# Query tiles with two blocks ahead, even slots of maxima, and a first phase loaded from the stage ahead

## The reference

```python
h = tok(x, ...)                       # attention in shifted 4x4 windows, 8 heads, with a relative table
h = h + attn(layernorm(h), ...)       # full attention over all 3136 tokens of an image, 8 heads of 32:
    q, k, v = split(x @ qkv_w + qkv_b)
    attn = softmax(einsum('bnhd,bmhd->bhnm', q * scale, k) + bias[rel_idx])
    out = einsum('bhnm,bmhd->bnhd', attn, v) @ proj_w + proj_b
h = h + ffn(layernorm(h), ...)        # gelu feed-forward for the half of the tokens with the top gate values
```

## Time and profile before

| | |
|---|---|
| median of 3 runs | 6077.67 us (6074.65 to 6080.56) |
| profiled execution | 6058.31 us, its span 6056.4 us |
| TensorE busy in the span | 5790.5 us (96%) |
| VectorE busy | 4380.1 us (72%) |
| GpSimd busy | 4386.0 us (72%) |
| ScalarE busy | 3273.6 us (54%) |
| mean granted clock of TensorE | 0.979 of 2.4 GHz |
| products for scores (line 1141) | 5600 |
| products for maxima (line 1205) | 5600 |

### The profile page before, as it was taken

How to read it: one execution, slowest core, us unless ns; L and a number is a source line. 1 busy time by engine, 2 the same in 40 slices (tenths; PEclk the granted TensorE clock), 3 DMA queues, 4 the chain that set the end, 5 groups by cost and what they waited for, 6 DMA issues and landing times. The chain is left out here.

```text
span 6056.4 us, 121185 instructions
## 1 busy us (share of the span) xinstructions
PE 5790.5 (96%) x37698; PEld 3429.1 (57%) x37698; DVE 4380.1 (72%) x8484; ACT 3273.6 (54%) x6740; POOL 4386.0 (72%) x1475
## 2 busy tenths in 40 slices
PE   5999998999999999999999999999999999984899
PEld 4777776555555555555555555555555555533566
DVE  4777776777877777777777777777777777736540
ACT  3555454266666666666666666666666666652222
POOL 2444444588888888888888888888888888875453
PEclk9999999799999999999999999999999999997899
DMA  2323223211011111101101110111111000015442
GB/s 73 100 93 105 95 98 112 62 35 37 16 37 33 28 25 37 36 17 37 33 27 25 37 36 17 37 33 27 25 37 36 16 17 17 15 31 160 119 98 44
DMA packets 197572, 297.79 MB, mean 49 GB/s; under 512 B 38038, under 2 KB 162334, under 8 KB 193998
## 3 DMA queue, kind: packets, MB, share of 16 engines
q1 hardware_dynamic: 181958, 269.42, 15.8%
q0 software_dynamic: 12432, 19.38, 1.6%
q10 hardware_dynamic: 2680, 2.63, 0.1%
HBM read 167.63 MB, written 124.50 MB: 48 GB/s over the span
## 5 line engine op out<-in xcount | busy, mean ns | idle before, releaser
L1302 DVE TENSOR_REDUCE tops<-ps_m 128x1 f32<-128x448 f32 (+1 forms) x5600 | 3116.7, 616 | 899.3 <-PE ps_m L1205 863.5
L1278 ACT ACTIVATE prob<-ps_s 128x448 f32<-128x448 f32 (+1 forms) x5600 | 2613.1, 548 | 1739.3 <-PE ps_s L1141 1696.8
L1111 POOL TENSOR_TENSOR tile_sum<-prob 128x1792 f32<-128x1792 f32 x448 | 1803.2, 4025 | 647.2 <-ACT prob L1278 646.8
L1141 PE MATMUL ps_s<-queries,keys 97*128 97x448 f32 (+1 forms) x5600 | 2197.3, 397 | 12.5 <-ACT prob L1278 7.6
L1205 PE MATMUL ps_m<-keys,queries 96*128 96x448 f32 (+1 forms) x5600 | 2090.1, 380 | 28.1 <-DMA keys<-k_parts 25.6
L1111 POOL TENSOR_TENSOR tile_sum<-tile_sum,prob 128x1792 f32<-128x1792 f32 x448 | 1808.0, 4036 | 31.8
L1141 PEld LDWEIGHTS ps_s<-queries,keys 97*128 97x128 f32 (+1 forms) x5600 | 1041.4, 187 | 1152.9 <-ACT prob L1278 661.4
L1157 PE MATMUL ps_o<-prob,values 128*32 128x448 f32 x11200 | 1341.8, 551 | 3.0 <-ACT prob L1278 1.2
L1205 PEld LDWEIGHTS ps_m<-keys,queries 96*128 96x128 f32 (+1 forms) x5600 | 1061.2, 190 | 234.1 <-DVE tops L1302 89.5
L1157 PEld LDWEIGHTS ps_o<-prob,values 128*32 128x32 f32 x11200 | 226.5, 108 | 379.4 <-issue 245.0
L1169 PE MATMUL ps_d<-tile_sum,ones 128*32 128x448 f32 x3584 | 420.9, 541 | 3.3 <-POOL tile_sum L1111 3.3
(11 more groups left out here) (181 smaller groups left out, 4096.3 us busy)
## 6 DMA issues: line engine op xcount, KB each, us to landing
queries<-q_parts SPq DMA_DIRECT2D x288, 160.0 KB, 3.3
keys<-k_parts SPq DMA_DIRECT2D x96, 392.0 KB, 7.1
xT<-in_x SPq DMA_DIRECT2D x56, 224.0 KB, 2.6
hidden_and_bias<-base SPq DMA_DIRECT2D x28, 448.0 KB, 3.1
q_parts<-hi SPq DMA_DIRECT2D x56, 224.0 KB, 1.9
q_parts<-lo SPq DMA_DIRECT2D x56, 224.0 KB, 1.9
k_parts<-hi SPq DMA_DIRECT2D x56, 224.0 KB, 1.9
k_parts<-lo SPq DMA_DIRECT2D x56, 224.0 KB, 1.9
```

The lines of the kernel that those rows point to most:

```text
L1111: nc.gpsimd.tensor_tensor(tile_sum[k % 2][:, :, :], left, prob[:, t % SLOTS, :, :], ALU.add).then_inc(summed, 1)
L1141: mm = nc.tensor.matmul(o[:, 0:CH], keys[x.u][:, j, at:at + k], queries[x.v][:, j, own:own + CH], start=True, stop=not last, skip_group_ch ...
L1278: nc.scalar.activation(prob[0:k, t % SLOTS, j, :], ps_s[0:k, score_bank(x.hm, i), 0:CH], ACT.Exp).then_inc(exp_done, 1)
L1302: nc.vector.tensor_reduce(tops[0:rows, j, r - blocks[0], c:c + 1], ps_m[0:rows, e % MB, 0:CH], AX.X, ALU.max).then_inc(m_used, 1)
```

## The change

It has two parts.

1. The tile of queries is 6 blocks wide, four of its own and `MORE` = 2 ahead; the first two blocks of a group are done for all four heads from the tile ahead, the others pair by pair. The spills are 8, 24, 12, 28, 16, 32 and 20, which gives 100 maxima to every slot (80 to the last of the last phase). The opening fill has 120 maxima instead of 122.
2. Keys, queries and corner of the first phase are allocated outside the two stages (`FirstPhase`), and SP loads them in the windowed stage: in round 27 the queries behind job 0, the corner behind job 1, and the keys of heads 0 and 1 behind jobs 2 and 3; in round 28 the keys of heads 2 and 3 behind jobs 0 and 1. The attention stage loads only the values itself. To make room, `ident` is gone; the first 128 columns of `out[0]` serve to make `ident_r`, and the turns' transposes read `ident_r`.

The diff, cut to its core:

```diff
+BLK = 128
+OWN, MORE = 4, 2
+AHEAD = (OWN + MORE) * BLK
...
+            def first_queries(pair):
+                rows = slice(2 * pair * DH, 2 * (pair + 1) * DH)
+                for row, part in ((0, 0), (DH, 0), (2 * DH, 1)):
+                    sp.dma_start(first.queries[row:row + DH, 2 * pair:2 * pair + 2, :].bitcast(F32),
+                                 d.q[0, part, rows, 0:AHEAD].rearrange("(j d) n -> d j n", j=2)
+                                 ).then_inc(first.q_in[pair], 16)
+
+            def first_corner():
+                sp.dma_start(first.corner_hi[:, :, :].bitcast(F32), d.corner[0, :, 0]).then_inc(first.corner_in, 16)
+                sp.dma_start(first.corner_lo[:, :, :].bitcast(F32), d.corner[0, :, 1]).then_inc(first.corner_in, 16)
+
+            def first_keys(j):
+                for row, part in ((0, 0), (DH, 1), (2 * DH, 0)):
+                    sp.dma_start(first.keys[row:row + DH, j, :].bitcast(F32),
+                                 d.k[0, part, j * DH:(j + 1) * DH, 0:N]).then_inc(first.k_in[j], 16)
+
+            def first_phase(m, job):
+                if m == ROUNDS - 1:
+                    if job == 0:
+                        for i in range(2):
+                            sp.wait_ge(parts_out[i], ONE + 16 * QK * PER_IMAGE)
+                        first_queries(0)
+                        first_queries(1)
+                    elif job == 1:
+                        first_corner()
+                    else:
+                        first_keys(job - 2)
+                elif m == ROUNDS and job < 2:
+                    first_keys(2 + job)
...
                     for job in range(1, QK):
                         parts(m - 2, job)
+                        if last or not units:
+                            first_phase(m, job)
...
-SPILLS = [10, 22, 10, 22, 10, 22, 16]
+SPILLS = [8, 24, 12, 28, 16, 32, 20]
...
-        entries += [("max", s, blocks[0], j, c) for j in range(HG) for c in range(PER_IMAGE)]
+        entries += [("max", s, r, j, c) for r in blocks[:MORE] for j in range(HG) for c in range(PER_IMAGE)]
         for p in range(2):
-            entries += [("max", s, r, j, c) for r in blocks[1:] for j in (2 * p, 2 * p + 1) for c in range(PER_IMAGE)]
+            entries += [("max", s, r, j, c) for r in blocks[MORE:] for j in (2 * p, 2 * p + 1) for c in range(PER_IMAGE)]
             entries.append(("turn", s, p))
...
-                    sp.dma_start(queries[1 - x.v][row:row + DH, :, 4 * BLK:5 * BLK].bitcast(F32),
-                                 d.q[x.g, part, :, bass.ds(x.b * N, BLK)].rearrange("(j d) n -> d j n", j=HG)
+                    sp.dma_start(queries[1 - x.v][row:row + DH, :, OWN * BLK:AHEAD].bitcast(F32),
+                                 d.q[x.g, part, :, bass.ds(x.b * N, MORE * BLK)].rearrange("(j d) n -> d j n", j=HG)
                                  ).then_inc(ahead_in, 16)
...
             first = Half(FIRST_ROUND, 0)
-            load_queries(first)
-            load_keys(first, 0)
-            load_corner(first)
-            for j in range(1, HG):
-                load_keys(first, j)
             load_values(first)
...
-                ahead = r == GROUP_BLOCKS[group][0] and not very_first
+                ahead = r in GROUP_BLOCKS[group][:MORE] and not very_first
...
-                if j % 2 == 0 and c == 0 and r == (0 if very_first else GROUP_BLOCKS[group][1]):
+                if j % 2 == 0 and c == 0 and r == (0 if very_first else GROUP_BLOCKS[group][MORE]):
                     pe.wait_ge(q_in[v][j // 2], ONE + 24 * (y.h - y.v) + 48)
```

More of the change, by code:

```diff
@@ L153, in _, with __init__, windows_and_qkv @@
                                     ALU.subtract).then_inc(lo_set, 1)
-def windows_and_qkv(nc, d):
+class FirstPhase:
+    def __init__(self, nc, ctx):
+        sb = lambda n, s: ctx.enter_context(nc.sbuf_tensor(n, s, F32R))
+        sem = lambda n: ctx.enter_context(nc.semaphore(n))
+        self.keys = sb("keys0", [STACK + 1, HG, N])
+        self.queries = sb("queries0", [STACK + 1, HG, AHEAD])
+        self.corner_hi = sb("corner_hi3", [128, HG, BLK])
+        self.corner_lo = sb("corner_lo3", [128, HG, BLK])
+        self.k_in = [sem(f"k_in0_{j}") for j in range(HG)]
+        self.q_in = [sem(f"q_in0_{pair}") for pair in range(2)]
+        self.corner_in = sem("corner_in3")
+        self.sems = [*self.k_in, *self.q_in, self.corner_in]
+def windows_and_qkv(nc, d, first):
     with ExitStack() as ctx:
@@ L862, in max_entries, with full_attention @@
     return entries, slots
-def full_attention(nc, d):
+def full_attention(nc, d, first_phase):
     with ExitStack() as ctx:
@@ L874, in sem @@
             return sems[-1]
-        keys = [sb(f"keys{u}", [STACK + 1, HG, N], F32R) for u in range(2)]
-        queries = [sb(f"queries{u}", [STACK + 1, HG, AHEAD], F32R) for u in range(2)]
+        keys = [first_phase.keys, sb("keys1", [STACK + 1, HG, N], F32R)]
+        queries = [first_phase.queries, sb("queries1", [STACK + 1, HG, AHEAD], F32R)]
         values = [sb(f"values{u}", [128, KT, HG * DH]) for u in range(2)]
-        corner_hi = sb("corner_hi3", [128, HG, BLK], F32R)
-        corner_lo = sb("corner_lo3", [128, HG, BLK], F32R)
+        corner_hi, corner_lo = first_phase.corner_hi, first_phase.corner_lo
         prob = sb("prob3", [128, SLOTS, HG, CH])
         tile_sum = [sb(f"tile_sum{i}", [128, HG, CH]) for i in range(2)]
-        ident = sb("ident3", [128, 128])
         ident_r = sb("ident_r", [128, 128], F32R)
@@ L901, in full_attention @@
             sem("id_zero3"), sem("id_set3"), sem("idr_set"), sem("ones_set3"), sem("rows_set"), sem("tops_set"))
[L902 removed]
+        k_in = [first_phase.k_in, [sem(f"k_in1_{j}") for j in range(HG)]]
         v_in = [sem(f"v_in{u}") for u in range(2)]
[L904 to L905 removed]
+        q_in = [first_phase.q_in, [sem(f"q_in1_{pair}") for pair in range(2)]]
+        corner_in, ahead_in = first_phase.corner_in, sem("ahead_in")
         shift_in = [sem(f"shift_in{p}") for p in range(2)]
@@ L1083, in _ @@
         def _(pool):
-            nc.gpsimd.memset(ident[:, :], 0.0).then_inc(id_zero, 1)
+            nc.gpsimd.memset(out[0][:, 0:128], 0.0).then_inc(id_zero, 1)
             pool.wait_ge(id_zero, ONE + 1)
-            nc.gpsimd.affine_select(out=ident[:, :], in_=ident[:, :], compare_op=ALU.not_equal, fill=1.0, base=0,
-                                    pattern=[[-1, 128]], channel_multiplier=1).then_inc(id_set, 1)
+            nc.gpsimd.affine_select(out=out[0][:, 0:128], in_=out[0][:, 0:128], compare_op=ALU.not_equal, fill=1.0,
+                                    base=0, pattern=[[-1, 128]], channel_multiplier=1).then_inc(id_set, 1)
             pool.wait_ge(id_set, ONE + 1)
-            nc.gpsimd.tensor_copy(ident_r[:, :], ident[:, :]).then_inc(idr_set, 1)
+            nc.gpsimd.tensor_copy(ident_r[:, :], out[0][:, 0:128]).then_inc(idr_set, 1)
             pool.wait_ge(idr_set, ONE + 1)
@@ L2009, in vit_tower @@
     setup_tables(nc, d)
-    windows_and_qkv(nc, d)
-    full_attention(nc, d)
+    with ExitStack() as ctx:
+        first_phase = FirstPhase(nc, ctx)
+        windows_and_qkv(nc, d, first_phase)
+        full_attention(nc, d, first_phase)
     gated_ffn(nc, d)
```

11 lines of the change are left out of this document (5 added, 6 removed).

## The result

The changed kernel takes 6040.98 us (median of 4 runs, 6036.71 to 6045.59) against 6076.16 us (6074.03 to 6080.56) for the kernel before: a ratio of 0.9943, 95% interval 0.9930 to 0.9955, 35 us less. 6048.6 had been forecast, with a range of 6038 to 6064. The direction and both mechanisms held; the gain is 6 us larger than the 29.1 us of the sum.

The account below looks back on a forecast made before the run. TensorE was taken to bound the attention halves, key arrivals and then VectorE the seam's fill. Preload -17.3 us and slots -11.8 made -29.1, taking 6077.7 us to 6048.6, range 6038 to 6064.

Parts of the forecast that it names:

- Preload: Seam before the attention stage: earlier start 10.4 us, three gaps 6.3, two maxima fewer 1.1, less 0.5 lost; 17.3 us net.
- Loss at the end of the windowed stage: Last rounds of the windowed stage: stores queue behind preloaded keys, costing 0.5 us, with bounds 0 and 6.
- the seven semaphores counted up a stage earlier: Moved increments, on engines said to wait at the seam anyway: costed at nothing.
- Slots: Attention halves: 100 maxima in every slot, -15.4 us over phases 0 to 6, +3.6 in the last; -11.8 us.
- the fifth entry: Tiles of attention halves: a fifth entry costs 0.48 us; two halves per phase have six such tiles fewer.
- the larger step: Halves going from 108 to 102 entries save 3.40 and 3.10 us, kept as the bound of -17 us.
- missing entries give nearly nothing: Last phase's last filled half, from 92 entries to 82: taken as 0, between -0.3 and +0.5 us.
- none at 79: Sign expected in the changed profile: halves at 76.0 us, those with corners up to 77.0, none at 79.
- (1): Windowed stage's last rounds: stores behind keys pay the preload back, about 10.5 us instead of 0.5; 6058.6 us, chance 0.13.
- (4): Windowed stage's last rounds: all 6.5 MB lies serially ahead of awaited stores, 58 us; 6106 us, slower, chance 0.04.
- (2): Attention halves: even slots bring nothing, their term at 0; 6060.4 us, chance 0.11.
- (3): Seam: something beside the keys held the first products, fill unchanged; -11.8 us alone, 6065.9 us, chance 0.04.

Follow-up runs that it names:

- after_again: The changed kernel run and profiled a second time, no edit: 6040.43 us, ratio 0.9939 to the kernel before.
- extra_after_sum: Changed kernel with each half's two left-over entries put behind bursts of sums instead of directly behind another entry: 6018.42 us, ratio 0.9900 to the kernel before.
- after: The changed kernel's first measurement and profile, against the kernel before: 6040.98 us, ratio 0.9943.
- after_third: The changed kernel run a third time, no edit, in a later set of runs: 6022.44 us against 6062.49 for the kernel before, ratio 0.9936.
- late_preload: Changed kernel with all 20 preloading DMAs put into round 28, behind jobs 0 and 1: 6046.41 us, ratio 0.9971 to the kernel before of its set.
- slots_only: Changed kernel with the loads of queries, keys and corner put back at the seam, new slots kept: 6056.12 us, ratio 0.9968 to the kernel before.
- preload_only: Changed kernel with the old slots and spills put back, preload kept: 6057.27 us, ratio 0.9967 to the kernel before.

## Why the prediction was right, and where its sizes were off

The time lies in the range, 7.6 us under the forecast, and both mechanisms are what the profiles show. The forecast was short on both terms.

**Preload, 17.3 us net forecast, 18.7 measured** (92.85 to 74.19 us, with the windowed stage unchanged). First reduction at the end of the memset: right to 0.1 us. No gaps: right. Two maxima fewer: 1.0 us for 1.1. Loss at the end of the windowed stage: 0.5 us forecast, 0.1 measured in the first profile. In `after_again` and `extra_after_sum` the last two rounds took 1.5 us more, and the first cast of the last round waited 6.1 and 6.0 us for a store instead of 4.6; that is inside the bounds, and 0.1 us is not the whole range of this placement. The larger part of the difference is a step that I had put at nothing: the seven semaphores counted up a stage earlier. VectorE does 31 of these increments at the seam instead of 38, one each 0.1 us, and everything at the seam waits for them; the first work comes 7.35 us behind the last store instead of 8.0. The reason given there, that these engines wait at the seam anyway, was wrong: at the seam VectorE's increments are what the others wait for.

**Slots, -11.8 us forecast, -17.2 measured** (-17.9 with the slots alone), just past the end of -17 that I gave. The term mis-sized is the fifth entry. I took 6 x 0.48 = 2.9 us for each of the two long halves; they lost 3.3 and 3.0 us, the value of the larger step, which I had kept as a bound. The halves that grew did so by less than the 1.20 us that I read from two rounded windows: 1.1 us in two of them, 0.7 in the one with the corner. A common phase so loses 3.6 us (535.9 to 532.3) instead of 2.2. The last phase paid 1.5 us instead of 3.6: its last filled half, with 82 entries, became 0.7 us shorter, where I had allowed 0.3. The reading that missing entries give nearly nothing compared that half with halves of other phases.

That the sum still came out near its bound is luck. Seven common phases and the last one alone would be -23.7 us, and two things that the prediction doesn't have gave 6 us of it back. In the halves at the return of the hardware loop (14, 15, 28 and 29) the profile lost some 5 us. TensorE stands still for 2.3 us ahead of the first score of halves 15 and 29, 1.8 to 2.0 us before, for nothing that the profile names. These halves scatter: half 15 takes 76.4, 77.4 and 79.1 us in the three profiles with the old slots. Why they grew is open. And half 0 grew by 1.7 us instead of 0.7. Of the granted clock of 0.50 the prediction says that it leaves the sum alone, which holds for the fill, but not for half 0 behind it. The prediction's sign "none at 79" is broken by half 29 (79.4 us); it says nothing against the mechanism, since it stands at the loop's return.

**Costed at nothing:** the wider query DMAs, and the shift rows of the later pair at a spill of 8. In the changed profile scores wait for shift rows once, 1.2 us at half 55, as before. The wider DMAs show no cost with the preload, but 0.9 us at the seam in the kernel with the slots alone.

**The profile against the median.** I took the 19.4 us between the profiled execution and the medians of before as a constant of the measurement. It went with the set of runs. For the kernel before there is no profile in the slower set, but for the changed one there is: `after` and `after_third` differ by 22.9 us in their spans, 15.4 of it in the last stage, 5.1 in half 55 and 3.2 ahead of the first score, less 0.9 in the halves. It did no harm, since the sum was carried to the median as a difference.

**Rivals.** (1) is excluded for this placement and shown to be real for another: `late_preload` pays 17.6 us. The 58 us of (4), which has the same place, were not seen even there. (2) is excluded by `slots_only`, and (3) by `preload_only` and by the landings of the keys.

## What to carry to other kernels

Preload the next stage's data in the gaps between stores of the stage ahead, a piece for each gap: the same bytes cost 0.1 to 1.5 us spread over six gaps and 17.6 us in two, because the stores queue behind them. Where one engine feeds another through a few banks, even counts are not enough: put the odd extra product behind a burst of other work, while the consumer catches up (0.31 us for 0.48), and look at what the shifted order does to entries that wait for something else, as the turn did here. And read a change's gain stretch by stretch, since the whole spans of two profiles may differ by the set of runs as much as by the change.

## What the runs showed of the hardware

- The same kernel took 6076 us in one set of runs and 6063 in others, with 647 to 654 us against 636 to 642 in its last stage, at the same mean granted clock there (0.89 or 0.90). The ratio of two kernels stayed within 0.0007.
- TensorE's granted clock fell to 0.50 for 13.7 us near the start of half 55 in four of the five profiles taken where the kernel before takes 6076 us, and in none of the others. In the first of them TensorE had been busy for 73.6 of the 74.8 us of the half before. It was standing idle for 1.2 us as the clock fell, as it did in the profiles where the clock stayed. It cost 5.1 us.
- Behind the seam the granted clock came back to 1.00 between 4.1 and 9.8 us after the first score, and half 0 took 75.8 to 78.3 us with it, for one and the same order of entries.
- Two stores issued behind 6.5 MB of loads in the same queue (4.1 MB, then 2.4 more) landed 14.1 and 22.0 us after their issue, 0.8 us behind the last load ahead of each.
- Semaphore increments on VectorE came 0.1 us apart, and 31 to 38 of them stand in series at the attention stage's start.
